# Reordering the first microseconds of a fused conditioning, feed-forward and low-rank kernel

## What is computed

```python
x = x + ffn0(cond0(x, lengths, conv_w), w_gate, w_up, w_down)   # masked mean, 5-tap conv, sigmoid gate; 8-bit activations, ternary weights
x = x + ffn1(cond1(x), W_base, b_base, lora_A, lora_B, router)  # dense, experts of rank 8, softmax over 4 of 16

def cond1(x, weight, scale_log, codebook, lora_A, lora_B):      # weight 512x512, rank 64
    lora_delta = lora_B @ lora_A * (32.0 / 64)
    cb = codebook / max(abs(codebook))                          # 8 entries
    scale = exp(scale_log)                                      # one per row and group of 128 columns
    normalized = ((weight + lora_delta) grouped) / scale
    thresholds = (cb[:-1] + cb[1:]) * 0.5                       # 7, not in order
    w = cb[searchsorted(thresholds, normalized)]
    return x @ (w * scale + lora_delta).T
```

## Time and profile before

| | us |
|---|---|
| median of 3 runs | 155.97 (154.81 to 156.15) |
| the profiled execution, as timed | 154.66 |
| its span in the profile | 152.9 |
| around the span | 1.76 |

### The profile page before, as it was taken

How to read it: one execution, slowest core, us unless ns; L and a number is a source line. 1 busy time by engine, 2 the same in 40 slices (tenths; PEclk the granted TensorE clock), 3 DMA queues, 4 the chain that set the end, 5 groups by cost and what they waited for, 6 DMA issues and landing times.

```text
span 152.9 us, 2333 instructions
## 1 busy us (share of the span) xinstructions
PE 141.7 (93%) x758; PEld 89.2 (58%) x758; DVE 113.8 (74%) x302; ACT 95.8 (63%) x163; POOL 11.0 (7%) x31
## 2 busy tenths in 40 slices
PE   6679999998799959999988999999999999999993
PEld 2256665753356736637636465565576766787792
DVE  2799999989999999999999767979893031035561
ACT  3899998996997966955827479786731403400200
POOL 7000000000000034100005200000000000000000
PEclk9999999999999999999999999999999999999999
DMA  5999999749500000000000000000000000000193
GB/s 166 389 406 417 417 419 399 272 154 392 194 0 0 0 2 4 0 0 0 4 0 0 0 0 6 0 0 2 0 4 0 0 0 0 0 4 0 61 373 115
DMA packets 6687, 16.06 MB, mean 105 GB/s; under 512 B 674, under 2 KB 1058, under 8 KB 6676
## 3 DMA queue, kind: packets, MB, share of 16 engines
q1 hardware_dynamic: 6676, 15.92, 27.5%
HBM read 13.82 MB, written 2.10 MB: 104 GB/s over the span
## 4 chain that ended last, share of the span: by engine, by line
PE 48%; DVE 29%; ACT 10%; issue 8%; DMA 2%; SPq 0%; ACTq 0%
PE bank L924 15%; PE bank L871 9%; ACT tern_d L491 6%; PE bank L837 6%; PE bank L843 6%; DVE hmax L1273 5%; DVE raw_gate L1270 5%; DVE junk L1109 2%; DMA cond<-in_cond_w 2%; DVE rmax L1159 2%; PE bank L882 2%; PE bank L856 2%; ACT cond L457 1%; PE bank L931 1%; DVE tern_i L1154 1%
## 5 line engine op out<-in xcount | busy, mean ns | idle before, releaser
L837 PE MATMUL bank<-tern_g,head_sb 128*128 128x464 bf16 (+1 forms) x96 | 22.5, 357 | 2.0 <-ACT head_sb L528 1.2
L843 PE MATMUL bank<-tern_u,head_sb 128*128 128x464 bf16 (+1 forms) x96 | 22.5, 357 | 0.0
L924 PE MATMUL bank<-m_h,fr 128*128 128x512 f32 (+1 forms) x72 | 22.3, 378 | 0.0
L871 PE MATMUL bank<-tern_d,delta 128*128 128x512 bf16 (+1 forms) x88 | 20.5, 379 | 0.3 <-ACT b_full L666 0.2
L592 ACT ACTIVATE raw_gate<-raw_gate,hq 128x1376 int16<-128x1376 f32 x8 | 11.5, 1440 | 13.0 <-DVE hq L1280 13.0
L1270 DVE TENSOR_TENSOR raw_gate<-bank,wbt 128x464 f32<-128x464 f32 (+1 forms) x24 | 15.1, 631 | 4.5 <-ACT wbt L585 4.4
L585 ACT ACTIVATE wbt<-bank,s_g 128x464 f32<-128x464 f32 (+1 forms) x24 | 15.3, 639 | 1.9 <-PE bank L837 1.9
L1273 DVE TENSOR_REDUCE hmax<-raw_gate 128x1 f32<-128x464 f32 (+1 forms) x24 | 15.1, 630 | 0.8
L750 PE MATMUL bank<-wbt,cond 128*128 128x512 f32 x32 | 14.8, 599 | 0.0
L843 PEld LDWEIGHTS bank<-tern_u,head_sb 128*128 128x128 bf16 x96 | 9.3, 98 | 9.2 <-DVE raw_gate L1270 0.2
L924 PEld LDWEIGHTS bank<-m_h,fr 128*128 128x128 f32 x72 | 13.2, 189 | 2.7
(11 more groups left out here) (174 smaller groups left out, 234.7 us busy)
## 6 DMA issues: line engine op xcount, KB each, us to landing
raw_gate<-in_w_gate_t SPq DMA_DIRECT2D x4, 688.0 KB, 7.6
raw_up<-in_w_up_t SPq DMA_DIRECT2D x4, 688.0 KB, 12.6
xs<-in_x SPq DMA_DIRECT2D x8, 256.0 KB, 13.0
out_x<-xs SPq DMA_DIRECT2D x7, 256.0 KB, 2.2
raw_down<-in_w_down_t SPq DMA_DIRECT2D x2, 768.0 KB, 5.4
cond<-in_cond_w SPq DMA_DIRECT2D x4, 256.0 KB, 4.4
wbt<-in_w_base_t SPq DMA_DIRECT2D x4, 256.0 KB, 9.6
raw_down<-in_w_down_t SPq DMA_DIRECT2D x2, 512.0 KB, 7.6
```

Source lines behind the costliest of these rows:

```text
L837: mm = pe.matmul(bank_g[n % 2][:, 0:w], xq_t[:, b % 2, k, :], tern_g[:, k, f0:f0 + w], start=(k == 0), stop=(k == KH - 1))
L843: mm = pe.matmul(bank_u[n % 2][:, 0:w], xq_t[:, b % 2, k, :], tern_u[:, k, f0:f0 + w], start=(k == 0), stop=(k == KH - 1))
L871: mm = pe.matmul(bank_down[:], h_t[0:rows, b % 2, j, :], tern_d[0:rows, j, :], start=(j == 0), stop=(j == KF - 1))
L924: pe.matmul(bank_y[n_res][:, h0:h1], a[:, b, k, :], m[:, k, h0:h1], start=(n == 0), stop=False)
```

## The change

It touches the head and a few places just behind it:

1. The first DMA carries only the 36 small columns of `head_sb`. The LoRA factors come as a second DMA, on 64 partitions, once instead of twice (`ld_lora`). The matmuls of the deltas read 64 rows, and `DELTA_FACTOR` is no longer halved.
2. `keep_clock` makes 5 dummy matmuls instead of 7. All four `lora_delta` stand ahead of `codebook(0)`.
3. GpSimd scales row block 1 in one `tensor_tensor` of 128 x 512 with the scales broadcast; ScalarE no longer does. It stands in GpSimd's list after the index patterns, and waits for the scales and for `cond` 1.
4. Each row block has its own semaphore. For block 0 VectorE waits group by group, for the others for the whole block.
5. The thresholds are ordered in two steps: the two inner ones ahead of `normalise(0)`, the outer ones after the second mask, with their last wait behind the third mask.
6. `M_ORDER = (1, 0, 2, 3)`: the fold's results are copied out in this order, `x_transposes(1)` waits for one copy instead of two, and `fold(3, 3)` goes ahead of `gate_up(0, 1)` instead of behind it.

```diff
-COPIES = P // RANK0
-DELTA_FACTOR = LORA0_FACTOR / COPIES
+DELTA_FACTOR = LORA0_FACTOR
-WARM_HEAD = 7
+WARM_HEAD = 5
+SCALED_BY_POOL = (1,)
+M_ORDER = (1, 0, 2, 3)
...
-        lora_a, lora_bt = lora_sb[:, 0, :], lora_sb[:, 1, :]
+        lora_a, lora_bt = lora_sb[0:RANK0, 0, :], lora_sb[0:RANK0, 1, :]
...
-            sp.dma_start(head_sb[:], head).then_inc(ld_head, 16)
+            sp.dma_start(head_sb[:, 2 * H:HEAD], head).then_inc(ld_head, 16)
+            sp.dma_start(head_sb[0:RANK0, 0:2 * H], lora0).then_inc(ld_lora, 16)
             for k in range(KH):
-                sp.dma_start(cond[:, k, :], cond_v[:, k, :]).then_inc(ld_cond[k], 16)
+                load_cond(k)
...
             pool.memset(ones[:], 1.0).then_inc(iota_done, 1)
+            for k in SCALED_BY_POOL:
+                pool.wait_ge(inv_done, 1)
+                pool.wait_ge(ld_cond[k], 16)
+                pool.tensor_tensor(cond[:, k, :].rearrange("p (g i) -> p g i", g=KH),
+                                   cond[:, k, :].rearrange("p (g i) -> p g i", g=KH),
+                                   scl_inv[:, k, :].unsqueeze(2).broadcast_to([P, KH, GROUP]),
+                                   ALU.mult).then_inc(condn_done[k], 1)
...
                 for g in range(KH):
                     c = slice(g * GROUP, (g + 1) * GROUP)
-                    ins = act.activation(cond[:, k, c], cond[:, k, c], ACT.Copy, scale=scl_inv[:, k, g:g + 1])
-                ins.then_inc(condn_done, 1)
+                    act.activation(cond[:, k, c], cond[:, k, c], ACT.Copy,
+                                   scale=scl_inv[:, k, g:g + 1]).then_inc(condn_done[k], 1)
...
-            for n, i in enumerate(T_ORDER):
+            for i in T_ORDER:
                 diagonals(i)
-                if n == 3:
-                    scaled_weight(1)
...
             def m_copy(k):
                 act.wait_ge(fold_ps, k + 1)
-                if k == 0:
+                if k == M_ORDER[0]:
                     act.wait_ge(tern_out, 2 * NC - 1)
...
-                    for k in range(KH):
+                    for k in M_ORDER:
                         m_copy(k)
...
-            pe.wait_ge(ld_head, 16)
-            lora_delta(0)
-            lora_delta(1)
+            pe.wait_ge(ld_lora, 16)
+            for k in range(KH):
+                lora_delta(k)
...
             codebook(0)
-            lora_delta(2)
-            lora_delta(3)
             codebook(1)
...
                 if b == 1:
-                    pe.wait_ge(mfull_done, 2)
+                    pe.wait_ge(mfull_done, M_ORDER.index(1) + 1)
...
                 gate_up(b, 0)
+                if b == 0:
+                    fold(KH - 1, 3)
...
                 gate_up(b, 1)
                 if b == 0:
-                    fold(KH - 1, 3)
                     conv(1)
...
-            def ordered_thresholds():
+            def inner_thresholds():
                 dve.tensor_tensor(t(1), t(1), t(3), ALU.min)
-                link(dve.tensor_tensor(t(5), t(5), t(3), ALU.max))
+                dve.tensor_tensor(t(5), t(5), t(3), ALU.max).then_inc(th_done, 1)
+
+            def outer_thresholds():
+                dve.wait_ge(th_done, 1)
                 dve.tensor_tensor(t(0), t(0), t(1), ALU.min)
                 dve.tensor_tensor(t(6), t(6), t(5), ALU.max)
                 dve.tensor_scalar(t(2), t(2), t(1), t(3), ALU.max, ALU.min)
-                link(dve.tensor_scalar(t(4), t(4), t(3), t(5), ALU.max, ALU.min))
+                dve.tensor_scalar(t(4), t(4), t(3), t(5), ALU.max, ALU.min).then_inc(th_done, 1)
 
             def normalise(k):
 
-                dve.wait_ge(condn_done, k + 1)
+                if k > 0:
+                    dve.wait_ge(condn_done[k], 1 if k in SCALED_BY_POOL else KH)
...
                 for g in range(KH):
                     c = slice(g * GROUP, (g + 1) * GROUP)
+                    if k == 0:
+                        dve.wait_ge(condn_done[k], g + 1)
...
+            inner_thresholds()
             normalise(0)
-            masks(0, 0, 1)
-            ordered_thresholds()
-            masks(0, 1)
+            masks(0, 0, 2)
+            outer_thresholds()
+            masks(0, 2, 3)
+            dve.wait_ge(th_done, 2)
+            masks(0, 3)
             normalise(1)
...
+        "lora0": np.concatenate([n(L1_cond_lora_A), n(L1_cond_lora_B).T], axis=1),
         "head": np.concatenate([
-            np.tile(np.concatenate([n(L1_cond_lora_A), n(L1_cond_lora_B).T], axis=1), (P // RANK0, 1)),
```

More of the change, by code:

```diff
@@ L75, with build @@
 SUMMED_BY_ACT = 3
-def build(nc, x, head, w_gate_t, w_up_t, w_down_t, cond_w, w_base_t, b_base,
+def build(nc, x, head, lora0, w_gate_t, w_up_t, w_down_t, cond_w, w_base_t, b_base,
           lora1, router, conv_band, out):
@@ L259, in build @@
         ld_head, ld_exp, ld_router, ld_band = sem("ld_head"), sem("ld_exp"), sem("ld_router"), sem("ld_band")
+        ld_lora = sem("ld_lora")
         ld_cond = [sem(f"ld_cond{k}") for k in range(KH)]
@@ L271, in build @@
         delta_ps = sem("delta_ps")
-        condn_done = sem("condn_done")
+        condn_done = [sem(f"condn_done{k}") for k in range(KH)]
         norm_done = sem("norm_done")
@@ L275, in build @@
         step_done = sem("step_done")
+        th_done = sem("th_done")
         b_full_done = sem("b_full_done")
@@ L366, in load_wbase, with load_cond @@
                 sp.dma_start(wbt[:, k, :], wbase_v[:, k, :]).then_inc(ld_wbase[k], 16)
-            sp.dma_start(head_sb[:], head).then_inc(ld_head, 16)
+            def load_cond(k):
+                sp.dma_start(cond[:, k, :], cond_v[:, k, :]).then_inc(ld_cond[k], 16)
+            sp.dma_start(head_sb[:, 2 * H:HEAD], head).then_inc(ld_head, 16)
+            sp.dma_start(head_sb[0:RANK0, 0:2 * H], lora0).then_inc(ld_lora, 16)
             for k in range(KH):
-                sp.dma_start(cond[:, k, :], cond_v[:, k, :]).then_inc(ld_cond[k], 16)
+                load_cond(k)
             sp.dma_start(rwp[:], router).then_inc(ld_router, 16)
@@ L548, in m_high @@
             def m_high(k):
-                act.wait_ge(mfull_done, k + 1)
+                act.wait_ge(mfull_done, M_ORDER.index(k) + 1)
                 act.activation(m_h[:, k, :], m_full[:, k, :], ACT.Copy).then_inc(mh_done, 1)
```

## The result

| | before | after |
|---|---|---|
| median (range), 4 runs each | 156.06 us (154.81 to 156.20) | 158.87 us (158.41 to 159.01) |
| the profiled execution, as timed | 154.66 | 158.95 |
| its span | 152.9 | 157.2 |

The ratio is 1.0207, with a 95% interval of 1.0156 to 1.0258. The forecast was 154.7 us, in a range up to 156.0: wrong in sign and outside its range. A ratio is not the quotient of the two medians beside it (here that is 1.018), and it leaves out executions that took over 1.5% more than the fastest of the same kernel, which the medians and ranges keep.

The account below looks back on a forecast made before the run. ScalarE and VectorE were taken to bound the kernel; the smaller of their gains, 1.26 and 1.25 us, came off the median of 155.97 us to give 154.7 us, range 153.7 to 156.0.

Parts of the forecast that it names:

- seam: VectorE's read of ScalarE's convolution result, line 1120, after 0.36 us idle: to come at 31.7 us instead of 32.93.
- TensorE's term: In the head: four deltas of 0.86 us end at about 8.1 us, codebook matmuls at 11.4, hidden by 1.2 us.
- the last rival: Slower: TensorE stays at its lower clock in the head; a rise at 12.4 us costs 1.6 us, 157.6 us; chance 0.08.
- The load to 64 partitions: In the head: factors at 243 GB/s land at 4.2 us, `cond` 0 at 4.9; ScalarE starts 0.1 us later.
- the router's rate: Lower end for the factors' load: 130 GB/s, from a 16-partition load; factors land at 5.15 us, ScalarE loses 0.9 us.
- normalise(0): VectorE's step in the head, to start at 5.6 us instead of 6.26: 0.66 us gained.
- The thresholds: VectorE's ordering between the first masks, 0.89 us before, partly moved under a wait: 0.44 us gained.
- The clash with GpSimd: GpSimd's scaling of block 1, 1.15 us long, holds up VectorE's first mask by 0.3 us (0 to 0.8).
- The scaling: Scaling row block 1 leaves ScalarE's list in the head: 1.16 us gained.
- Behind the head: After the head the gain is handed on to the end; the new fold order and earlier transposes count 0 us.
- The 1.3 us between the median and the profiled execution: In the sum: the median 155.97 us lies 1.3 us above the profiled execution; added to 153.4 to give 154.7.

Follow-up runs that it names:

- With the clock repaired: The changed kernel with 9 dummy matmuls instead of 5: median 155.03 us, ratio 0.9934 against before.
- the fill: 4 + 4 dummy matmuls in TensorE's two idle stretches near 53 and 56 us, alone in the kernel before: 154.74 us, ratio 0.9950.

## Why the prediction was wrong

The kernels that differ in the rows of the deltas and in the dummies, all with the change unless it says before:

| rows of the deltas | dummies | rise in the profiled execution, by the trace's list | seam | median |
|---|---|---|---|---|
| 64 | 5 (after) | 15.30 | 36.01 | 158.87 |
| 64 | 7 | 5.15 | 31.84 | 155.11 |
| 64 | 9 | 4.03, in the dummies | 32.05 | 155.03 |
| 128 | 5 | 10.32 | 33.53 | 155.67 |
| 128 | 9 | 5.43 | 32.01 | 154.49 |
| 128, before | 7 | 4.49 | 32.93 | 156.06 |
| 128, before | 5 | 7.38 | 32.97 | 156.61 |
| 64, before | 7 | 4.12, falls at 7.54, back at 14.36 | 35.51 | 157.80 |

**The step that failed** is TensorE's term, and with it the chance of the last rival. The term had four deltas of 0.86 us that end at 8.1, and a codebook hidden by 1.2 us: the full clock from the second delta on. They ended at 12.0, and `value(0)` waited 3.27 us for the codebook. The last rival named this, and its mechanism, its place and its price were right: half a microsecond for each one at the lower level behind 9.2 us. With the rise at 15.3 that is (15.3 - 9.2) x 0.5 = 3.05 us, and the seam moved by 3.08; with 128 rows it is 0.56, and the seam moved by 0.60. That the first comes out so close is in part luck: the 9.2 was worked out for deltas that start at 4.2, and they started at 4.81, while `value(0)` moved by 3.63 us, of which 0.55 was made up again ahead of the seam. What failed was where the rise could come: I let it be at 7.6, or at 12.4 at worst, and gave all of it 0.08. The prediction's own text had the reasons for more. It saw that the clock rose early in the first deltas after 3 us of dummies without a break, and that the change took away 0.9 us of those and put an idle stretch behind them. It priced the four deltas as if that didn't matter: they took 7.19 us, not 3.9. And it did not ask what matmuls on half of the rows do to the level. The earlier trace rows had no such row. The experiments say that it counts: with 5 dummies the rows are worth 5 us of the rise and 2.48 us at the seam, where four more dummies are worth 3.96, and by themselves they cost 1.2% in before.

**The load to 64 partitions.** I took 243 GB/s, between 394 and the router's 130, and 4.2 us for the landing; it landed at 4.77. SyncE's timeline in after:

```profile
1.16 0.54 SPq L375 DMA_DIRECT2D head_sb<-in_lora  x1
1.74 2.00 SPq L372 DMA_DIRECT2D cond<-in_cond_w  x4
```

Its loads, from issue to landing:

```profile
head_sb<-in_lora SPq DMA_DIRECT2D x1, 256.0 KB, 3.6
...
head_sb<-in_head SPq DMA_DIRECT2D x1, 18.0 KB, 1.8
```

`cond` 0 is issued at 1.74 us, not 1.60, since the issue ahead of it takes 0.54 us. It lands at 5.24 and ScalarE starts at 5.34: 0.46 us lost instead of 0.1. The rule of the Trainium skill, "SBUF — State Buffer", Door 1: The DMA port swizzle, was the better guide than my interpolation: by it halving the bytes wins no time, and the traces agree, 3.6 us for 256 KB to 64 partitions and 3.6 for 512 KB to 128. The estimate by the Trainium skill, 1.2 us and so a landing at 4.35, was still 0.4 us early. The lower end of the range was also added up wrong: at the router's rate ScalarE would start at 5.9, which loses 1.0 us and not 0.9. The late factors also lengthened the idle stretch behind the dummies from the 0.8 us that I saw to 1.29. The small transfer landed in 1.8 us, at 2.5, better than the 2.9 taken; but nothing was waiting for the constants by then.

**normalise(0)** was to come at 5.6. With the clock repaired it comes at 6.33, since `cond` 0 and delta 0 are both late; before it was 6.26. So 0.66 us of VectorE's gain was -0.07.

**The thresholds** were right: from `normalise(0)` to `normalise(1)` 4.83 us before, 4.45 after and 4.44 with nine dummies, 0.39 us for a predicted 0.44.

**The clash with GpSimd** cost VectorE nothing, for a predicted 0.3. GpSimd in after:

```profile
7.11 1.04 POOL L421 TENSOR_TENSOR cond<-cond,scl_inv 128x512 f32<-128x512 f32 x1 [5.10 <-DMA cond<-in_cond_w]
...
9.88 0.82 POOL L432 TENSOR_SCALAR two_row<-part 128x1 f32<-128x1 f32 x1
```

The multiplication took 1.04 us (1.15 predicted). It lay beside the later `normalise(0)`, which kept its 1.13 us, and was over at 8.15 where the masks began at 8.09. What did lie beside the masks were GpSimd's small instructions, and those paid: `two_row` took 0.82 us, and 0.23 at 3.02 us in before. The masks kept 0.41 us each. Whether the multiplication would slow a mask was not met.

**The seam** was right as a place, and its gain too large. With nine dummies VectorE's own list gains 0.32 us at `normalise(1)` and `value(0)`, 0.44 from `value(1)` (17.56 to 17.12) to `value(3)` (31.82 to 31.38), and 0.88 at line 1137, where the wait of 0.36 goes as well. The forecast had 0.8, 0.9 and 1.25. VectorE's is the shorter gain: ScalarE's result `ycond` is there at 31.84, and VectorE reaches it at 32.05 without a wait. The scaling was worth at least 1.08 us to ScalarE (1.16 predicted).

**Behind the head** was right: what is won or lost at the seam is there at the next `ytiny` (after 3.06 late of 3.08, nine dummies 0.90 early of 0.88), and the fold order is worth nothing.

**The 1.3 us between the median and the profiled execution**, carried along in the sum as if it were a constant, was the fall of the clock, absent from the one profile that I had: it goes with a mean clock of 0.989, and the fill takes both away. No execution of before that has the fall was profiled; in the profiles that have it, it starts between 55.2 and 59.7 us.

**Open.** What sets the moment of the rise: the kernel with two deltas ahead of the codebook came between both theories. Why 64 rows leave some executions late even with nine dummies (two of ten there, three of ten at 158.9 or more where ScalarE scales block 1). By the Trainium skill, "TensorE: Matmul & The Clock Gate", Part 1, the moment of the rise varies from run to run. The traces agree: with the same nine dummies and 64 rows it was at 4.03 in one kernel and at 5.14 in the one where ScalarE scales block 1, and with 128 rows at 5.43, 4.90 and 5.24 in three. The Trainium skill gives some 0.5 us either way there. The late executions (159.3 us with seven dummies, 159.2 with nine) take as long as those of after, whose rise was at 15.30; by that, as an estimate, theirs would be some 10 us later than the others'. None of them was profiled. And whether the change makes the fall near 60 us more frequent: it is in 35 of 67 executions of before, in 4 of 4 of after, in 10 of 10 on 128 partitions with 5 dummies, in 8 of 10 with nine dummies and in 5 of 10 with both.

## What to carry to other kernels

Before you shorten or move anything in the first microseconds of TensorE, find in the trace when its spacing halves, what lay ahead of that, and how late it may come before its reader waits. If an edit takes matmuls, rows or continuity out of what lies ahead, price the whole stretch at the lower level and give that case a real chance. Dummy matmuls ahead of the first real work are cheap (here four of them gave back 3.96 us), and a load that is halved by using half of the partitions needn't land any earlier. If the median lies over the profiled execution by more than the runs' own noise, look for a second mode in the clock of each run before you carry the difference along; a half-idle stretch of TensorE in the middle of the kernel is where to look.

## What the runs showed that I had not expected

- The granted clock's row reads 1.00 from the start, though the spacing of the same matmul halves at 15.4 us. The trace's list of changes begins with that rise, and the row takes what lies ahead of its first entry for 1.00. At the start of a kernel the level is to be read from the spacing. Later in the kernel the row does show a fall (0.50 between 60 and 62 us).
- Matmuls on 64 rows instead of 128, with the same columns, put the rise back by 5 us with 5 dummies, and in before let the level fall again at 8.2 us.
- Eight dummy matmuls in a stretch where TensorE was busy for 0.96 and 0.83 of 2 us each kept the clock at 0.998 or more in 21 of 21 executions. The idle pieces were only 1.04 and 1.17 us long.
- Small instructions of GpSimd take up to 0.82 us instead of 0.23 beside VectorE's masks, and VectorE pays nothing.
